# Gate and up of seven experts as Strassen's seven products over pairs of token blocks

## The reference

```python
weights = router(x)                                   # [b, t, 8], after a layer norm of x
gate = einsum('btd,edf->ebtf', x, Wg)                 # 8 experts, D = F = 512
up   = einsum('btd,edf->ebtf', x, Wu)
gate[:2] += einsum('btd,edr,erf->ebtf', x, Ga, Gb)    # low rank (64) for experts 0 and 1
up[:2]   += einsum('btd,edr,erf->ebtf', x, Ua, Ub)
mid = silu(gate) * up
out = einsum('ebtf,efd->ebtd', mid, Wd)               # + low rank Da, Db for experts 0 and 1
return x + einsum('bte,ebtd->btd', weights, out)
```

## Time and profile before

| | |
|---|---|
| median of 3 runs | 1139.37 us (1139.03 to 1140.16) |
| span of the profiled execution | 1137.2 us |
| own time of the profiled execution | not given apart from its span; the median is 2.2 us above the span |
| instructions | 13865 |
| PE busy | 1116.4 us (98%), 5016 matmuls |
| DVE busy | 383.2 us (34%) |
| ACT busy | 267.4 us (24%) |
| POOL busy | 204.1 us (18%) |
| DMA | 42.83 MB |

### The profile page before, as it was taken

One profiled execution on the slowest core, in us unless ns is written; L12 is line 12 of the kernel. 1 busy time (PEld: TensorE's weight loads), 2 busy tenths in 40 slices (PEclk: granted clock), 3 DMA queues, 4 the chain that ended last, 5 costly groups with the idle time before them and its releaser, 6 DMA issues.

```text
span 1137.2 us, 13865 instructions
## 1 busy us (share of the span) xinstructions
PE 1116.4 (98%) x5016; PEld 917.9 (81%) x5016; DVE 383.2 (34%) x679; ACT 267.4 (24%) x448; POOL 204.1 (18%) x172
## 2 busy tenths in 40 slices
PE   6899999999999999999999999999999999999998
PEld 4687787888888888888888888888888888888886
DVE  6888785311131112311132112422323222321111
ACT  3454253211131112211132111312122112311111
POOL 2511121111111111111111111122111122111111
PEclk9999999999999999999999999999999999999999
DMA  8310003200020000300002000210003000000001
GB/s 298 122 47 1 1 1 112 112 1 0 0 74 37 0 0 0 111 0 0 0 17 94 0 0 0 110 39 18 0 1 129 18 18 0 0 1 37 37 37 37
DMA packets 23014, 42.83 MB, mean 38 GB/s; under 512 B 2128, under 2 KB 2256, under 8 KB 22992
## 3 DMA queue, kind: packets, MB, share of 16 engines
q1 hardware_dynamic: 22704, 42.49, 10.6%
q10 hardware_dynamic: 288, 0.07, 0.0%
HBM read 38.36 MB, written 4.19 MB: 37 GB/s over the span
## 4 chain that ended last, share of the span: by engine, by line
PE 96%; DVE 2%; DMA 1%; ACT 1%; issue 0%; POOL 0%; DVEq 0%
PE gate_up L1020 20%; PE gate_up L1021 20%; PE gate_up L1026 20%; PE tiles L954 10%; PE tiles L952 10%; PE tiles L953 10%; PE tiles L985 1%; DMA w_raw<-in_xT_dram 1%; PE tiles L977 1%; PE tiles L1049 0%; PE tiles L1048 0%; PE gate_up L970 0%; PE gate_up L977 0%; ACT zt L484 0%; PE gate_up L960 0%
## 5 line engine op out<-in xcount | busy, mean ns | idle before, releaser
L1020 PE MATMUL gate_up<-xT_hi,w_hi 128*128 (+2 forms) x1056 | 403.5, 384 | 1.1 <-ACT xT_hi L490 0.8
L1021 PE MATMUL gate_up<-xT_hi,w_lo 128*128 (+2 forms) x1056 | 401.6, 383 | 0.0
L349 POOL TENSOR_TENSOR mid_lo<-mid,mid_hi 128x512 fp32r<-128x512 f32 (+1 forms) x132 | 166.8, 1263 | 876.1 <-ACT mid_hi L444 876.1
L1026 PE MATMUL gate_up<-xT_lo,w_hi 128*128 (+2 forms) x1056 | 254.1, 383 | 0.9 <-DVE xT_lo L629 0.9
L770 DVE TENSOR_TENSOR mid<-silu,gate_up 128x512 f32<-128x512 f32 (+1 forms) x132 | 88.5, 671 | 443.7 <-ACT silu L439 443.6
L1020 PEld LDWEIGHTS gate_up<-xT_hi,w_hi 128*128 128x128 f32 x1056 | 198.5, 188 | 40.8 <-issue 2.2
L1021 PEld LDWEIGHTS gate_up<-xT_hi,w_lo 128*128 128x128 f32 x1056 | 198.5, 188 | 39.3 <-issue 0.7
L1026 PEld LDWEIGHTS gate_up<-xT_lo,w_hi 128*128 128x128 f32 x1056 | 194.5, 188 | 39.8 <-DVE xT_lo L629 1.1
L439 ACT ACTIVATE silu<-gate_up 128x512 f32<-128x512 f32 (+1 forms) x132 | 77.1, 584 | 630.8 <-PE gate_up L1026 630.8
L952 PE MATMUL tiles<-w_hi,mid_hi 128*128 128x512 f32 x512 | 199.5, 390 | 0.0
L954 PE MATMUL tiles<-w_hi,mid_lo 128*128 128x512 f32 x512 | 199.2, 389 | 0.0
(11 more groups left out here) (112 smaller groups left out, 384.7 us busy)
## 6 DMA issues: line engine op xcount, KB each, us to landing
w_raw<-in_wg_dram SPq DMA_DIRECT2D x7, 1024.0 KB, 5.2
w_raw<-in_wu_dram SPq DMA_DIRECT2D x7, 1024.0 KB, 7.5
w_raw<-in_wd_dram SPq DMA_DIRECT2D x7, 1024.0 KB, 5.3
w_raw<-in_xT_dram SPq DMA_DIRECT2D x4, 1024.0 KB, 6.1
out_dram<-xacc SPq DMA_DIRECT2D x16, 256.0 KB, 2.1
xacc<-in_x_dram SPq DMA_DIRECT2D x3, 1024.0 KB, 5.8
lora_a<-in_loraT_dram SPq DMA_DIRECT2D x12, 128.0 KB, 2.8
lora_b<-in_lora_dram SPq DMA_DIRECT2D x12, 128.0 KB, 2.8
```

Of the source, the lines that this page charges most:

```text
L349: nc.gpsimd.tensor_tensor(mid_lo[:, f, tokens], mid[:, f % 2, tokens], plain(mid_hi[:, f, tokens]), ALU.subtract).then_inc(lo_made, 1)
L1020: nc.tensor.matmul(dst, w_hi[:, m, k, cols], xT_hi[:, k, tok], start=(k == 0), stop=False)
L1021: nc.tensor.matmul(dst, w_lo[:, m, k, cols], xT_hi[:, k, tok], start=False, stop=False)
L1026: ins = nc.tensor.matmul(gate_up[:, 2 * p + m, tokens], w_hi[:, m, k, cols], xT_lo[:, k, tok], start=False, stop=(k == KT - 1))
```

## The change

**The products.** The transposed weight matrix of gate or up (features x D) and the transposed activations (D x tokens) are cut into 2 x 2 quarters. One *quad* is two feature tiles (f and f + 2) by two token blocks, with D in two halves of 256. In place of eight quarter products it takes Strassen's seven (in Winograd's form), each of two 128-deep slices by three passes: six matmuls. They go to three banks: products 1, 6, 7, 4 accumulate one after another in a gate bank (0 or 3 in turn), 5 and 3 in bank 1, 2 in bank 2. In between the bank is copied by ScalarE: P1 to `s1_sb`, P5 to `p5_sb`, P1+P6 to `u2_sb`. The four outputs are C11 = P1 + P2, C12 = (P1+P6) + (P5+P3), C22 = P5 + (P1+P6+P7), each one VectorE add (`combine`), and C21 = P1+P6+P7+P4 in the bank itself.

**Sums of weights.** A *piece* is one quad's weights: four quarters of 128 x 256, loaded in rows of 512 B by two DMAs (0.5 MB). VectorE makes four sums of 256 columns from it (`piece_sums`), ScalarE rounds seven operands in one op of 1792 columns, VectorE makes the low parts in ops of 1024 and 768 columns. Three piece buffers rotate; a load waits for product 4 of three pieces before.

**Sums of activations.** Four sums of the pair's activations (1024 columns each) are made once per pair. For the first pair GpSimd first stages blocks 2 and 3 to DRAM (`stage`) and adds high and low parts (`x_sum`), VectorE makes four differences and four half low parts. For the second pair they are made at the swap from the staged copy: four differences, seven half low parts on VectorE, seven roundings on ScalarE.

**Order.** There are 14 steps: seven experts on token blocks 0 and 1, then the same seven on blocks 2 and 3 (the second pair's `xacc` waits in DRAM meanwhile). A step is four quads (gate f = 0, 1, up f = 0, 1), with the two halves of the down projection of the step before between them, and product 4 of a quad delayed past the first part of what follows. In step 0 no down halves lie between the quads; before step 7 both halves stand ahead of its first quad.

**Low rank.** The six merged matrices are made in steps 0 to 5, written to DRAM, and loaded from there in both passes (before, they were merged in place in SBUF, one position ahead of their use).

**Loops.** All of it is written out; the hardware loops are gone.

The core of the diff:

```diff
@@ block.tensor
+            def product(j, i, dst, first=False, last=False):
+                hi, lo = piece_hi[j % 3], piece_lo[j % 3]
+                for kt in range(2):
+                    cols = slice(kt * P, (kt + 1) * P)
+                    w_h, w_l = hi[:, COMBO[i] - 1, cols], lo[:, COMBO[i], cols]
+                    x_h, x_l = x_operand(i, kt)
+                    nc.tensor.matmul(dst, w_h, x_h, start=first and kt == 0, stop=False, skip_group_check=True)
+                    nc.tensor.matmul(dst, w_l, x_h, start=False, stop=False, skip_group_check=True)
+                    ins = nc.tensor.matmul(dst, w_h, x_l, start=False, stop=last and kt == 1, skip_group_check=True)
+                ins.then_inc(p_mm[i], 1)
...
+            def quad(j, pending):
...
+                product(j, 1, gate_bank(j), first=True)
+                reach(pe, c_made[C12], j)
...
+                product(j, 5, gate_up[:, BANK_B, :], first=True)
+                if pending:
+                    fourth(j - 1)
+                pe.wait_ge(s1_made, j + 1)
...
+                product(j, 6, gate_bank(j))
+                pe.wait_ge(p5_made, j + 1)
...
+                product(j, 3, gate_up[:, BANK_B, :], last=True)
+                reach(pe, c_made[C11], j)
...
+                product(j, 2, gate_up[:, BANK_C, :], first=True, last=True)
+                pe.wait_ge(u2_made, j + 1)
...
+                product(j, 7, gate_bank(j))
...
-            with pe.Fori(1, PLAIN - 1) as s:
-                with pe.Fori(0, B) as b:
-                    for f in range(FT):
-                        gate_and_up(s, b, f)
-                    all_down(s, b)
...
+            for k in range(STEPS):
+                j = 4 * k
+                if k == SWAP:
+                    down_half(k - 1, 0, j - 1)
+                    down_half(k - 1, 1, None)
+                if k in (0, SWAP):
+                    quad(j, False)
+                    quad(j + 1, True)
+                    quad(j + 2, True)
+                else:
+                    quad(j, True)
+                    down_half(k - 1, 0, j)
+                    quad(j + 1, False)
+                    down_half(k - 1, 1, j + 1)
+                    quad(j + 2, False)
+                if k < len(LORA_JOBS):
+                    low_rank(k)
+                quad(j + 3, True)
+            down_half(STEPS - 1, 0, 4 * STEPS - 1)
+            down_half(STEPS - 1, 1, None)
@@ block.scalar, the loop over steps k, j = 4 * k
+                elif k == 0:
+                    piece_high_part(1)
+                else:
+                    mid_high_part(k - 1, 1, C12)
+                copy_p1(j)
+                if k not in (0, SWAP):
+                    mid_high_part(k - 1, 1, C11)
+                    mid_high_part(k - 1, 1, C22)
+                copy_p5(j)
+                if k not in (0, SWAP):
+                    piece_high_part(j + 1)
+                    mid_high_part(k - 1, 1, C21)
+                copy_u2(j)
...
+                    copy_p1(j + 2)
+                    copy_p5(j + 2)
+                    piece_high_part(j + 4)
+                    copy_u2(j + 2)
+                wd_high_part(k)
+                for c in (C12, C11, C22):
+                    mid_high_part(k, 0, c)
+                copy_p1(j + 3)
+                copy_p5(j + 3)
+                if k in (0, SWAP):
+                    piece_high_part(j + 4)
+                mid_high_part(k, 0, C21)
+                copy_u2(j + 3)
@@ block.vector, the same loop
+                if k > 0:
+                    combine(k - 1, UP, 1, C22)
+                    make_mid(k - 1, 1, C11)
+                    make_mid(k - 1, 1, C22)
+                    piece_sums(j + 1)
...
+                elif k > 0:
+                    make_mid(k - 1, 1, C21)
+                    piece_low_part(j + 1)
...
+                    add_down(k - 1, 1)
+                    piece_sums(j + 4)
+                    if k < len(LORA_JOBS):
+                        lora_a_low_part(k)
+                    piece_low_part(j + 4)
...
+                combine(k, UP, 0, C12)
+                combine(k, UP, 0, C11)
+                make_mid(k, 0, C12)
+                combine(k, UP, 0, C22)
+                make_mid(k, 0, C11)
+                make_mid(k, 0, C22)
+                if k < len(LORA_JOBS):
+                    add_lora(k)
+                wd_low_part(k)
+                if k in (0, SWAP):
+                    piece_sums(j + 4)
+                make_mid(k, 0, C21)
...
+                combine(k, UP, 1, C12)
+                combine(k, UP, 1, C11)
+                make_mid(k, 1, C12)
@@ block.vector, ahead of step 0
+            t_low_part(1, 5)
...
+            t_low_part(3, 6)
+            t_low_part(2, 7)
+            t_low_part(4, 4)
+            piece_sums(1)
             dve.wait_ge(rw_ready, B)
             accumulate(B - 1, B - 1, 0)
...
+            piece_low_part(1)
@@ block.vector, at k == SWAP, behind four differences and seven half low parts
+                    add_down(k - 1, 0)
+                    piece_sums(j + 2)
+                    piece_low_part(j + 2)
+                    add_down(k - 1, 1)
@@ block.gpsimd
+            x_sum(0, 1, 0)
+            x_sum(1, 0, 0)
+            low_part(B - 1, 2)
+            x_sum(2, 1, 2)
+            low_part(B - 1, 3)
+            pool.wait_ge(t_made, 2)
+            x_sum(0, 0, 2)
+            for k in range(STEPS):
+                if k < len(LORA_JOBS):
+                    lora_b_low_part(k)
+                for m in range(2):
+                    for c in (C12, C11, C22, C21):
+                        mid_low_part(k, m, c)
```

More of the change, by code:

```diff
@@ L32 @@
 BLOCK_CREDIT = 4
-LORA_CREDIT = 4
 GOLDEN_CENTER = 1.0 / math.e
@@ L53 @@
 SIM_BANK = [2, 3, 0, 1]
+STEPS = 2 * (POSITIONS - 1)
+SWAP = POSITIONS - 1
+GATE, UP = 0, 1
+BANK_B, BANK_C = 1, 2
+COMBO = {1: 2, 2: 3, 3: 7, 4: 1, 5: 4, 6: 5, 7: 6}
+C12, C11, C22, C21 = 0, 1, 2, 3
+DOWN_ORDER = (0, 2, 1, 3)
+LORA_JOBS = ((0, 2), (0, 0), (0, 1), (1, 2), (1, 0), (1, 1))
 HALF = S // 2
@@ L87, in xattn_ffn_kernel @@
[L87 to L99, removed]
+        arena_at = nc.sbuf_base + (-nc.sbuf_base) % 32
@@ L311, in _ @@
+            for i in range(2 * TT):
+                store_out(2 * TT + i, 8 * (STEPS - 1) + i + 1)
             sp.wait_ge(stored, 16 * B * TT)
@@ L595, in _ @@
+            for c in (C12, C11, C22, C21):
+                mid_high_part(STEPS - 1, 1, c)
         @block.vector
@@ new lines, in piece_low_part, with wd_low_part @@
+            def piece_low_part(j):
+                if j >= 4 * STEPS:
+                    return
+                dve.wait_ge(piece_hi_made, j + 1)
+                for first, last in ((1, 5), (5, 8)):
+                    ins = nc.vector.tensor_tensor(piece_lo[j % 3][:, first:last, :], piece[j % 3][:, first:last, :],
+                                                  plain(piece_hi[j % 3][:, first - 1:last - 1, :]), ALU.subtract)
+                ins.then_inc(piece_ready, 1)
+            def wd_low_part(k):
+                dve.wait_ge(wd_hi_made, k + 1)
+                for h in range(2):
+                    part = slice(2 * h, 2 * h + 2)
+                    ins = nc.vector.tensor_tensor(wd_lo[:, part, :], wd_raw[:, part, :], plain(wd_hi[:, part, :]),
+                                                  ALU.subtract)
+                ins.then_inc(wd_ready, 1)
@@ new lines, in add_down, with difference @@
+            def add_down(k, h):
+                b, s = 2 * (k // SWAP) + h, 1 + k % SWAP
+                for t in range(TT):
+                    dve.wait_ge(d_mm, 8 * k + 4 * h + t + 1)
+                    nc.vector.scalar_tensor_tensor(tile_of(b, t), tiles[:, t, :],
+                                                   rw[:, (b * TT + t) * E + s:(b * TT + t) * E + s + 1], tile_of(b, t),
+                                                   ALU.mult, ALU.add).then_inc(d_added, 1)
+            def difference(to, left, right):
+                nc.vector.tensor_tensor(to, left, right, ALU.subtract).then_inc(t_made, 1)
@@ L945, in _ @@
+            combine(STEPS - 1, UP, 1, C22)
+            make_mid(STEPS - 1, 1, C11)
+            make_mid(STEPS - 1, 1, C22)
+            make_mid(STEPS - 1, 1, C21)
+            add_down(STEPS - 1, 0)
+            add_down(STEPS - 1, 1)
         @block.tensor
```

652 lines of the change are left out of this document (467 added, 185 removed).

## The result

The changed kernel takes 1149.1 us (median of 4 runs, 1147.9 to 1149.5); the kernel before took 1139.3 beside it. The ratio of the times is 1.0084, with an interval of 1.0072 to 1.0096: 0.8% slower, 6 us above the forecast of 1143. 336 matmuls are gone, and the time is not shorter.

A forecast was written before the change was run, and what follows sets the result against it. TensorE, busy without a break, bounds the kernel before; after the change latency decides. 1139.4 - 76.2 (matmuls) + 43 (steps) + 18.6 + 1.5 (start) + 15.3 + 1.5 (swap) = 1143.1 us, range 1098 to 1166.

The forecast's parts named there:

- The matmuls: On TensorE after the first expert, 336 matmuls go at 0.2267 us each, saving 76.2 us; 3744 remain.
- The lock: A GpSimd op holds off a VectorE op with two SBUF inputs, costing its dense row 1.05 us each time.
- rival 1: GpSimd does not get into VectorE's rows: steps lose 16, start 14, swap 14, giving 1107 us; chance 0.30.
- A steady step: Waits of TensorE for late copies: 4.05 us per plain step, 2.9 per lora step, 43 us over twelve steps.
- (a): First quad of a step: product 7 waits for the late copy of P1+P6, 1.8 us lost.
- (b): Fourth quad of a step: product 6 waits for the late copy of P1, 1.3 us lost.
- (c): Fourth quad of a step: product 7 waits for the late copy of P1+P6, 0.95 us lost.
- The start: Product 6 of the first quad 12.6 us late, 6 more in step 0: 18.6, plus 1.5 for clock.
- The swap: Step 7: the second half of down waits 12.3 us for adds, 3 more later: 15.3, plus 1.5 for clock.
- The clock: Granted clock drops around gaps: 1.5 us each at start and swap; gaps under 2 us cost zero.
- Transfers: Loads of a piece take 4 to 7.4 us against 8.9 available between issue and use, so they stay hidden.
- rival 2: Pieces land late (11 us or more) or small gaps lower the clock: 24 us more, 1167; chance 0.10.

The follow-up runs named there:

- experiment 1: Changed kernel with GpSimd's low part of each mid cut from 512 columns to 64, the down projection reading the high part instead (output differs): 1100.6 us.
- experiment 5: Changed kernel with VectorE's sums, low parts and down-weight split moved behind the combines TensorE waits for, and ScalarE copying before rounding, within each step: 1112.1 us.
- experiment 2: Changed kernel with ScalarE's copy of P1+P6 in each step's first quad ahead of rounding the next piece and mid C21: 1146.4 us.
- experiment 4: Changed kernel with, at the swap, mid C21 made and rounded earlier and the down projection's adds ahead of seven half low parts: 1137.7 us.
- experiment 6: Changed kernel with copies of P1 and P5 ahead of piece rounding in early quads of steps 0 and 7, and piece 1 summed earlier: 1147.4 us.
- experiment 7: Changed kernel with the reorderings of experiment 4, experiment 5 and experiment 6 together: 1097.5 us.
- experiment 3: Changed kernel with ScalarE's copies of P1 and P1+P6 in each step's fourth quad ahead of rounding mids: 1156.3 us.
- experiment 8: On experiment 7, quad 2's copy of P1+P6 ahead of rounding piece 3 in steps 0 and 7, piece 3 loaded before the first lora loads: 1095.2 us.

## Why the prediction was right, point by point

**The matmuls.** Right: 3744 after the first expert, 0.2267 apart; TensorE never waiting would have been 1063, and stretches without a loss are there in experiments 1 and 5.

**The lock.** Right, and it carries the forecast. Predicted was 1.05 us per GpSimd op that meets VectorE, from the earlier trace rows; the 256-wide sums at 870.09 and 871.53 pay 1.10 and 1.09. With GpSimd's ops short the steady loss fell to 0.5 us and the time came near rival 1's (1100.6 against 1107). What rival 1 still had at 1.3 a step, the chain without the lock, measured nothing. The Trainium skill (SBUF — State Buffer, "SBUF: two separate sides") has it as an exclusive lock of the whole instruction. The trace agrees: the sum that starts at 870.09 ends at 871.61, 0.28 us after the GpSimd op that ran beside it (869.65 to 871.33).

**A steady step.** Right in place, size and releaser. (a) 1.8 before product 7 of the first quad: 1.7. (b) and (c), 1.3 and 0.95 in the fourth quad: 2.0 together. Plain step 4.05: 3.7. Lora step 2.9: 2.1; there the low-rank matmuls cover more than (b). 43 predicted, 38.9 measured.

**The start.** The gaps were predicted at 18.6 and are 17.3 in step 0, but not all where they were placed. A part of the first 12.6 stands before product 5 (3.56, `tx_lo`), the rest before product 6 (5.35), where 10 or more were predicted; and quad 2 waits 4.1 before product 6 where 2.2 were predicted (see on transfers). The first product itself is 2.8 late, which was not in the sum. 1.3 of it is a wait of TensorE for `mid_low` (1.04) with its restart: that mid stands on VectorE behind the router, which GpSimd held, and behind a difference that lasted 3.41 us beside a GpSimd sum of 2.57. The other 1.5 was there at 186 us already, in a stretch with a granted clock of 0.96 where before it had 0.99, and the change is not shown to be its cause: in experiments 1, 2, 4, 6 and 7, with the same code up to there, the clock of that stretch is 0.99 and the first product starts at 209.4 to 209.7 instead of 210.98; in 3, 5 and 8 it starts at 210.7 to 211.4.

**The swap.** Right in mechanism: predicted one delay of 12.3 by the adds and 3 later, measured a second half of the down projection that starts 11.9 late, and 9.2 lost from there on, with slow matmuls in both. 10.0 of the 11.9 are two gaps: the first for mid C21, inside the first half, which the prediction did not name as a wait of its own, the second for the adds. Experiment 4 moved these two and got 11.4 back.

**The clock.** Here is the term that was mis-sized: 1.5 at the start and 1.5 at the swap, against 6.9 and 5.0 measured (some 0.15 for each gap of it is plain restart). I read the price off, whose windows had 0.78 and 0.88; behind the gaps of 3.6 to 5.8 us the granted clock was about half for 2.3 to 5.7 us in which TensorE was fully busy. Gaps under 2 us were priced at zero, and in the steps of the changed kernel that held (1.00). The 7.1 by which the losses were forecast too low are 8.9 of the clock, 2.8 of the late first product, 0.8 of the swap's gaps, less 1.3 at the start and 4.1 in the steps; the median lies 1.3 above the span instead of 2.2, which leaves 6. So two errors stand against each other: the losses of the steps and the gaps of the start were forecast 5.4 too high, which hid a part of what the clock cost; the total would otherwise have missed by more, so its nearness is in part luck.

**Transfers.** Right in the main: a piece's two halves land in 3.2 and 3.3 us each (medians), well under 7.4, and product 1 waits for none (rival 2). But one load was late in the way that rival 2 named. Piece 3 is issued behind the first lora loads at 239.34 and has landed at 246.16; VectorE waits 2.56 for it (the longest of the two waits in `DVE piece L1073 <- DMA` above), ScalarE's rounding of the piece waits behind the sums, the copy of P1 behind the rounding, and that is the gap of 4.1 before product 6 of quad 2. The prediction had 2.2 for the wait at that place and took every load as hidden.

## What to carry to other kernels

When an edit trades matmuls for small operations on other engines, don't compare busy times; follow the one chain that must return to TensorE within a product or two, with all that stands ahead of each link in its in-order queue. Work for later goes where the engine idles, behind what TensorE waits for, on every engine of the chain. Moving only the last link forward did not pay: with the copy first in ScalarE's queue 2.7 us were gained in one place and 7.3 lost in the other: the wait came back behind VectorE's work, which had stayed, and in the second case the clock fell as well. With both moved, order alone turned 0.8% slower into 3.9% faster. Gaps can cost more than their length: in the changed kernel the granted clock was half behind each gap of 3.6 us and more.

## What the runs showed that I had not expected

The lock holds small operations as long as large ones: a router op on 32 columns took 2.32 us beside a GpSimd op of 2.39 that started before it, the second of the two in the first row, where its like takes 0.19. It ended 0.05 us after that op.

```profile
190.19 4.74 POOL L521 TENSOR_TENSOR tx_sum<-xT_hi,xT_lo 128x1024 f32<-128x1024 f32 x2
...
192.66 2.32 DVE L994 SCALAR_TENSOR_TENSOR w_zone<-z,w_zone 128x32 f32<-128x32 f32 x1
...
197.52 0.19 DVE L1006 SCALAR_TENSOR_TENSOR fb<-rank,fb 128x32 f32<-128x32 f32 x1
```

The granted clock does not follow from the longest gap alone. With gaps of up to 3.1 us it stayed at 1.00 in one stretch of the changed kernel (734 to 744 us), and in experiment 3 it was 0.97 over 190 us with none above 2.2. Even the same gap had both: 3.13 us before product 7 of quad 31, with the starts behind it at the full pace in the changed kernel and 0.43 apart, half the clock, in experiment 4. What decides between them is open.
